# Two heads side by side in the rows of the array: 56-row score products for even and odd heads in place of 72-row products, in an attention and feed-forward kernel on one core

## The reference

```python
x = x + attention(layernorm(x))      # 16 heads of 8 channels, causal,
                                     # T5 relative-position bias (32 buckets, largest distance 128)
x = x + ffn(layernorm(x))            # router fixed to expert 0: relu(t @ w1 + b1) @ w2 + b2,
                                     # residual, layernorm with gamma and beta
# attention: sim = q @ k.T + bias[bucket(i - j)] * scale, -inf above the diagonal; softmax; @ v
```

## Time and profile before

| | us |
|---|---|
| median of 3 runs | 368.16 (365.61 to 368.34) |
| the profiled execution's own time | 367.01 |
| span of its trace | 365.2 |
| PE busy | 326.3 |
| DVE busy | 273.8 |
| ACT busy | 190.4 |
| POOL busy | 65.5 |

### The profile page before, as it was taken

How to read it: one execution, slowest core, us unless ns; L and a number is a source line. 1 busy time by engine, 2 the same in 40 slices (tenths; PEclk the granted TensorE clock), 3 DMA queues, 4 the chain that set the end, 5 groups by cost and what they waited for, 6 DMA issues and landing times.

```text
span 365.2 us, 8215 instructions
## 1 busy us (share of the span) xinstructions
PE 326.3 (89%) x3233; PEld 155.1 (42%) x3235; DVE 273.8 (75%) x952; ACT 190.4 (52%) x262; POOL 65.5 (18%) x79
## 2 busy tenths in 40 slices
PE   8846886699999998998999999899999989999971
PEld 4323442242444354344434434444443443348741
DVE  5565374985777895887799589689969987547895
ACT  1340595134557536655754665574466557763330
POOL 4118999300000000000000000000000001432551
PEclk9985698957999999999999999999999999999997
DMA  7455317200202201020220123032112102000022
GB/s 203 138 176 134 82 46 242 82 4 1 66 2 66 61 9 46 24 66 1 68 63 7 52 48 93 2 90 73 31 55 48 24 3 39 9 2 16 0 57 58
DMA packets 13830, 20.89 MB, mean 57 GB/s; under 512 B 2944, under 2 KB 10240, under 8 KB 13664
## 3 DMA queue, kind: packets, MB, share of 16 engines
q1 hardware_dynamic: 13104, 17.28, 17.4%
q10 hardware_dynamic: 688, 3.09, 3.1%
HBM read 13.90 MB, written 4.23 MB: 50 GB/s over the span
## 4 chain that ended last, share of the span: by engine, by line
PE 58%; DVE 16%; ACT 14%; issue 5%; POOL 3%; DMA 2%; ACTq 1%; DVEq 0%; POOLq 0%
PE ps L1029 15%; PE ps L1072 15%; PE ps L1043 14%; ACT PT L647 10%; PE ps L1060 6%; DVE FM L783 4%; DVE junk L790 3%; PE ps L963 2%; ACT TT L605 2%; POOL XN L495 2%; PE ps L1105 2%; DVE st L858 1%; DVE U L911 1%; DMA qk_scratch<-QS 1%; DMA table_s<-in_table 1%
## 5 line engine op out<-in xcount | busy, mean ns | idle before, releaser
L647 ACT ACTIVATE PT<-ps 128x1024 f32<-128x1024 f32 (+1 forms) x192 | 145.6, 810 | 113.0 <-PE ps L1060 95.0
L783 DVE TENSOR_REDUCE FM<-ps 128x1 f32<-128x512 f32 (+3 forms) x176 | 108.2, 660 | 18.3 <-PE ps L1029 18.2
L790 DVE CUSTOM_DVE_ANT_0 junk<-ps,NBH 128x256 bf16<-128x256 f32 (+1 forms) x256 | 89.5, 403 | 33.9 <-PE ps L1029 33.7
L1029 PE MATMUL ps<-KA,QA 72*128 72x256 bf16 (+3 forms) x544 | 107.2, 291 | 2.2 <-DVE FM L783 1.0
L1043 PE MATMUL ps<-QA,KA 74*128 74x512 bf16 (+3 forms) x384 | 95.7, 334 | 11.1 <-ACT PT L647 9.7
L1072 PE MATMUL ps<-PT,VG 128*16 128x512 f32 (+3 forms) x768 | 86.9, 498 | 0.0
L1029 PEld LDWEIGHTS ps<-KA,QA 72*128 72x128 bf16 x544 | 43.9, 100 | 87.2 <-DVE FM L783 33.1
L541 POOL TENSOR_SCALAR tmp<-mv 128x4 f32<-128x4 f32 x8 | 2.3, 289 | 266.5 <-DVE mv L861 266.5
L1043 PEld LDWEIGHTS ps<-QA,KA 74*128 74x128 bf16 x384 | 31.9, 99 | 36.8 <-ACT PT L647 24.0
L1060 PE MATMUL ps<-TT,flb 128*32 128x176 f16 (+4 forms) x1152 | 38.5, 243 | 0.0
L1060 PEld LDWEIGHTS ps<-TT,flb 128*32 128x32 bf16 x1152 | 21.3, 96 | 17.5 <-issue 16.6
(11 more groups left out here) (93 smaller groups left out, 250.1 us busy)
## 6 DMA issues: line engine op xcount, KB each, us to landing
QA<-qk_scratch SPq DMA_DIRECT2D x48, 96.0 KB
KA<-qk_scratch SPq DMA_DIRECT2D x42, 96.0 KB
qk_scratch<-QS SPq DMA_DIRECT2D x8, 384.0 KB, 4.1
X<-in_x SPq DMA_DIRECT2D x4, 256.0 KB, 5.3
PT<-fr_scratch ACTq DMA_DIRECT2D x1, 1024.0 KB, 4.6
out<-U SPq DMA_DIRECT2D x4, 256.0 KB, 2.3
OT<-f_scratch ACTq DMA_DIRECT2D x2, 480.0 KB, 8.7
xnT<-OT SPq DMA_DIRECT2D x28, 32.0 KB
```

The lines of the kernel that those rows point to most:

```text
L647: nc.scalar.activation(PT[:, s % 3, 2 * q:2 * q + 2, off:off + w], ST[:, q, :, off:off + w], ACT.Exp).then_inc(s_exp, 1)
L783: nc.vector.tensor_reduce(FM[:, ib, heads[0]:heads[-1] + 1, piece], bank[:, 0:w * len(heads)].rearrange("p (h n) -> p h n", n=w), AX.X, AL ...
L790: last = nc.vector.tensor_tensor_reduce(junk[:, k % NSM, i, 0:w], bank[:, i * w:(i + 1) * w], nb[:, h, 256 - w:256], 1.0, NEG, ALU.add, AL ...
L1029: last = nc.tensor.matmul(bank[:, i * w + j - j0:i * w + j - j0 + n], QA[0:KS, p, ib // 4, h, (ib % 4) * 128:(ib % 4 + 1) * 128], KA[0:KS, ...
```

## The change

The rows of the products go from 72 and 74 to 56 and 58: seven of the nine pairs of parts (all three of q with the high and the middle part of k, and the high part of q with the low part of k), and the two maximum rows. Heads 0 and 2 of a group lie in rows 0 to 57, heads 1 and 3 in rows 64 to 121, so each of the two products of a pair uses its own 64-row half of the array. A unit now holds heads of one parity; two units, one of each parity, are one `job`, whose matmuls alternate between the halves and go to two PSUM banks. The job of units k and k+1 waits until unit k - 2 has been read. `NU` becomes 42 (40 units in 20 jobs, and two "m"). The number of DMAs for a half of q or k goes from 3 to 6, and of `move_m` from 1 to 2. `ones` fills all rows of half as many columns.

```diff
-ROWS = NPART * NPART * HD
-KS = ROWS
-MROW = ROWS
+HP = HG // 2
+KS = (NPART * 2 + 1) * HD
+MROW = KS
...
-                nh = min(HG, 512 // pw)
-                for h0 in range(0, HG, nh):
-                    out.append(("far", ib, list(range(h0, h0 + nh)), j0, pw, piece))
-        nh = HG if ib == 0 else 2
-        for h0 in range(0, HG, nh):
-            out.append(("near", ib, list(range(h0, h0 + nh))))
+                nh = min(HP, 512 // pw)
+                for q0 in range(0, HP, nh):
+                    for e in range(2):
+                        out.append(("far", ib, [2 * q + e for q in range(q0, q0 + nh)], j0, pw, piece))
+        for e in range(2):
+            out.append(("near", ib, [2 * q + e for q in range(HP)]))
...
+JOBS = [k for k in range(NU) if UNITS[k][0] == "m" or UNITS[k][2][0] % 2 == 0]
...
-QK_AT = {5: (0, 0), 6: (0, 1), 7: (1, 0), 8: (1, 1)}
+QK_AT = {6: ((0, 0), (0, 1)), 8: ((1, 0), (1, 1))}
...
         def load_q(eng, g, p, c):
-            for u in range(NPART):
-                eng.dma_start(QA[u * NPART * HD:(u + 1) * NPART * HD, p, c, :, :].rearrange("r h n -> r (h n)"),
-                              bass.AP(qk_d, g * GN + 2 * c * NPART * PN, [[HG * IC, HD], [PN, NPART], [1, HG * IC]])
+            at = g * GN + 2 * c * NPART * PN
+            for e in range(2):
+                for u in range(2):
+                    r0 = 64 * e + 24 * u
+                    eng.dma_start(QA[r0:r0 + 24, p, c, :, :].rearrange("r h n -> r (h n)"),
+                                  bass.AP(qk_d, at + e * HP * IC, [[HG * IC, HD], [PN, NPART], [1, HP * IC]])
+                                  ).then_inc(s_ldqk[p][c], 16)
+                eng.dma_start(QA[64 * e + 48:64 * e + KS, p, c, :, :].rearrange("r h n -> r (h n)"),
+                              bass.AP(qk_d, at + e * HP * IC, [[HG * IC, HD], [1, HP * IC]])
                               ).then_inc(s_ldqk[p][c], 16)
...
-                sp.dma_start(QA[MROW:MROW + 2, p, half, :, :], mrow[:, half, :]).then_inc(s_md[half], 16)
+                for e in range(2):
+                    r0 = 64 * e + MROW
+                    sp.dma_start(QA[r0:r0 + 2, p, half, :, :],
+                                 mrow[4 * e:4 * e + 4, half, :]).then_inc(s_md[half], 16)
...
+                pieces = [(i, h // 2, j, n) for i, h in enumerate(u[2]) for j, n in cuts]
+                pe.wait_ge(s_smf, NU * g + k + 2)
+                for m, (i, q, j, n) in enumerate(pieces):
+                    for e in range(2):
+                        last = nc.tensor.matmul(SM[:, (k + e) % NSM, i * w + j - j0:i * w + j - j0 + n],
+                                                QA[64 * e:64 * e + KS, p, ib // 4, q, (ib % 4) * 128:(ib % 4 + 1) * 128],
+                                                KA[64 * e:64 * e + KS, p, j // IC, q, j % IC:j % IC + n],
+                                                start=True, stop=True)
+                        if m == len(pieces) - 1:
+                            last.then_inc(s_smr, 1)
...
-                for h in range(2 * q, 2 * q + 2):
-                    last = nc.tensor.matmul(ST[:, q, h % 2, off:off + w],
-                                            KA[0:KST, p, jb // 4, h, (jb % 4) * 128:(jb % 4 + 1) * 128],
-                                            QA[0:KST, p, ic, h, off:off + w], start=True, stop=not near,
+                for e in range(2):
+                    last = nc.tensor.matmul(ST[:, q, e, off:off + w],
+                                            KA[64 * e:64 * e + KST, p, jb // 4, q, (jb % 4) * 128:(jb % 4 + 1) * 128],
+                                            QA[64 * e:64 * e + KST, p, ic, q, off:off + w], start=True, stop=not near,
```

More of the change, by code:

```diff
@@ L131, in places @@
     costs = [unit_cost(u) for u in UNITS]
-    out, own, done = {}, {}, 0.0
-    for u in range(NU):
-        at = t * (S_START + (S_END - S_START) * done / sum(costs[:-1]))
+    out, own = {}, {}
+    for u in JOBS:
+        at = t * (S_START + (S_END - S_START) * sum(costs[:u]) / sum(costs[:-1]))
         if u == NU - 1:
             at = t * M1_AT
-        done += costs[u]
         s, pos = next((s, pos) for c, s, pos in pts if c > at % t)
@@ L157, in places0 @@
     slots = [(s, pos) for s in range(FIRST_STEP[1] - 1) for pos in range(3)]
-    for u in range(OWN0 + 2, NU - 1):
-        own.setdefault(slots[(u - OWN0 - 2) * len(slots) // (NU - 3 - OWN0)], []).append(u)
+    for u in JOBS:
+        if OWN0 + 4 <= u < NU - 1:
+            own.setdefault(slots[(u - OWN0 - 4) * len(slots) // (NU - 5 - OWN0)], []).append(u)
     own[slots[-1]].append(NU - 1)
-    out[slots[-1]] = list(range(FIRST0))
+    out[slots[-1]] = [u for u in JOBS if u < FIRST0]
     slots = [(s, pos) for s in range(FIRST_STEP[1] - 1, NSTEP) for pos in range(3)]
-    for u in range(FIRST0, NEXT0):
-        out.setdefault(slots[(u - FIRST0) * len(slots) // (NEXT0 - FIRST0)], []).append(u)
+    for u in JOBS:
+        if FIRST0 <= u < NEXT0:
+            out.setdefault(slots[(u - FIRST0) * len(slots) // (NEXT0 - FIRST0)], []).append(u)
     return out, own
@@ L266, in build, with hidden @@
         tT = work[:, 10 * IC:12 * IC].rearrange("p (c n) -> p c n", c=2)
-        hid = [work[:, 0:4 * IC],
-               KA[:, 0:1, :, :, :].rearrange("p o c h n -> p (o c h n)").bitcast(F32)]
+        hid = [work[:, 0:4 * IC]] + [
+            a[:, 0:1, :, :, :].rearrange("p o c h n -> p (o c h n)").bitcast(F32) for a in (QA, KA)]
+        def hidden(c, f):
+            if c % 2 == 0:
+                return hid[0][:, f * IC:(f + 1) * IC]
+            return hid[1 + f // 2][:, (f % 2) * IC:(f % 2 + 1) * IC]
         R = [PT[:, 1, :, :], OT[:, 4:6, :].rearrange("p g (c n) -> p (g c) n", n=IC)]
@@ L798, in unit @@
                     nm = NM[:, half, :]
-                    m0, m1 = (MC[:, half, :, q, :] for q in range(2))
+                    m0, m1 = (MC[:, half, :, :, q, :] for q in range(2))
                     v = 4 * g + 2 * half
@@ L1007, in _, with job @@
                 task_flip(i)
-            def unit(g, p, k):
+            def job(g, p, k):
                 u = UNITS[k]
-                bank = SM[:, k % NSM, :]
-                pe.wait_ge(s_smf, NU * g + k + 1)
                 if u[0] == "m":
-                    half = u[1]
+                    bank, half = SM[:, k % NSM, :], u[1]
+                    pe.wait_ge(s_smf, NU * g + k + 1)
                     pe.wait_ge(s_ms, 2 * g + half + 1)
@@ L1017, in unit @@
                         last = nc.tensor.transpose(bank.bitcast(BF16)[0:8, i * 128:(i + 1) * 128],
[L1018 removed]
+                                                   MC[:, half, i, :, :, :].rearrange("p e q h -> p (e q h)"), idb[:, :])
                     last.then_inc(s_smr, 1)
                     return
[L1021 removed]
+                ib = u[1]
                 if u[0] == "far":
@@ L1127, in s_units_at @@
                     for k in (OWN_UNITS0 if first else OWN_UNITS).get((s, pos), []):
-                        unit(g, p, k)
+                        job(g, p, k)
                     if not last:
@@ L1131, in s_units_at @@
                             if k in HALF_UNITS:
-                                pe.wait_ge(s_ldqk[1 - p][HALF_UNITS[k]], 96 * load)
-                            unit(g + 1, 1 - p, k)
+                                pe.wait_ge(s_ldqk[1 - p][HALF_UNITS[k]], LOADED * load)
+                            job(g + 1, 1 - p, k)
                 for s in range(NSTEP):
@@ L1165, in _ @@
             keep_busy(4, 6)
-            for k in range(OWN0):
+            for k in JOBS[:JOBS.index(OWN0)]:
                 if k in T_AT:
                     task_t(1, T_AT[k])
-                if k in QK_AT:
-                    task_qk(1, *QK_AT[k])
+                for c, qk in QK_AT.get(k, ()):
+                    task_qk(1, c, qk)
                 if k in V_AT:
@@ L1175, in _ @@
                 if k in HALF_UNITS:
-                    pe.wait_ge(s_ldqk[0][HALF_UNITS[k]], 96)
-                unit(0, 0, k)
+                    pe.wait_ge(s_ldqk[0][HALF_UNITS[k]], LOADED)
+                job(0, 0, k)
             pe.wait_ge(s_r, 4)
@@ L1184, in _ @@
                 scores(0, 0, 0, q)
-                unit(0, 0, OWN0 + q)
+                job(0, 0, OWN0 + 2 * q)
             biases(0, 0)
```

43 lines of the change are left out of this document (22 added, 21 removed).

## The result

The changed kernel takes 385.17 us (median of 4 runs, 380.66 to 388.10), the kernel before beside it 367.13. The ratio is 1.045, with a 95% interval of 1.035 to 1.056. The four runs differ in their clock: the mean granted one is 0.929 in the fastest and 0.905 in the slowest. The forecast was 378, with a range of 356 to 391.

What follows compares the result with a forecast made beforehand. PE bounded groups 1 to 5, DVE close. On 367.0 us: start-up +2.0, group 0 -3.0, groups 1 to 5 +3.3, group 6 +2.3, group 7 -2.0, clock +7.2 gave 376.8; 1.2 for the median: 378, range 356 to 391.

Steps and rivals of the forecast that it cites:

- the main case: SP's queue becomes the bound of a group and the clock falls behind it: 372 to 392 us; chance 0.50.
- That the halves don't overlap: Rival: PE's work stays, with the DMA wait on top; 33.5 us a group, 384 us; chance 0.08.
- That SP isn't late: Rival: the twelve DMAs land in time for PE; 30.2 us a group, 356 us (350 to 363); chance 0.18.
- The clock holds: Rival: same DMA wait, but no stretch of low clock; 371 us (365 to 373); chance 0.24.
- the pair's wait: Jobs 12 to 39: each waits until only one unit is unread; DVE starves 0.8 us (bounds 0 and 1.5).
- the walk: Jobs up to T (a group's first exponential), each at the later of PE's turn and its awaited unit; 15.3 us DVE work.
- The stop: PE stands still 2.8 us ahead of job 12 in each group until the twelfth load lands.
- The clock: Granted clock falls behind PE's standstill in each group: 1.2 us a group (ends 0 and 3.5), +7.2 in all.
- Start and group 0: Start-up +2.0 us for three more ACT DMAs; group 0 -3.0 us, its second half freed of PE's bound.
- Group 6: Four reciprocals on DVE, three of them behind the DMA wait: 35.0 us, +2.3, without the clock's 1.2.
- Group 7: No units; its chain runs through scores in 12 steps: -2.0 us (bounds -3 and 0).

Runs made afterwards that it cites:

- the dummies: Ten dummy products of 512 columns on PE ahead of job 12, ahead of the wait for the loads, in the changed kernel: 384.66 us.
- the torn biases: Biases of each pair right behind its scores: 351.23 us on the changed kernel with q loads first, jobs earlier, 7 start dummies; 385.62 us in the kernel before.

## Why the prediction was right, and where its numbers were not

**The mechanism and its place were right.** Twelve issues in 7.7 us behind two for the rows, PE standing still in front of job 12 until a DMA lands, a lower clock behind it, 34.2 us a group where the main case said 33.6 (31.76 + 0.65 + 1.2). The run with the q loads first takes the queue's stop away and gives 12 us back; the run with twice the DMAs puts it into the old kernel and costs 2.1 us in each group with a full clock.

**The rivals.** That the halves don't overlap is out: 0.34 us for two products of 384 columns. That SP isn't late is out as a description of the change; made true, it gives 373 and not the 356 worked out for it. "The clock holds" was true by itself in group 5, which takes 33.4 us where this rival had 32.4; with the dummies it was made true in nearly all groups, at the price of a later job 12, and gives 384.7 and not 371.

**The step that was mis-sized is the one on the pair's wait**, the walk from job 12 to the next T, where "DVE starves 0.1 to 0.3 us at four places, 0.8 in all", and with it the 30.2 us of a group whose loads are in time. That group takes 32.14. The way from job 12 to the next T, 17.1 us in the walk, is 18.3 in group 5 with the clock at 1.00; in group 2 it is 19.4 (159.01 to 178.44), of which the clock is 1.1. That leaves 1.2 us a group that the walk didn't have. Two edits show part of what the walk lacks: VectorE idle in the first steps (0.9 us came back by placing the jobs earlier), and ACT's chain through scores, jobs and biases (2.0 came back by the torn biases). My own reading of the rest, which no run isolates: the walk took each engine's work at its row, and let an engine start as soon as one other was ready; it never let ACT, DVE and PE each be a little late on the same step.

**The stop was over-sized.** The landing was T+14.7, not 15.3, since the issues for 8 rows take 0.46 us and not 0.65; PE came at T+13.3, not 12.5. So the stop is 1.5 us in this group (10.9 us in six), not 2.8. It lengthened a group by about 1.0 us (33.1 against 32.14: a landing at T+14.8 and 18.3 us behind it), where the forecast had 2.2 (32.4 against 30.2). **The clock was right in sum:** 1.1 to 1.2 us in each of groups 1 to 4, nothing in group 5 and 3.1 in group 6, together some 7.6 us where 7.2 were forecast. That it would hold in one group and stay down 10 us in another wasn't foreseen. The walk and the stop err in opposite ways, and it is luck that the sum of a steady group came out near: +2.4 a group measured, +1.85 forecast.

**Start and group 0 went the other way**, +4.8 against -1.0. ACT's three more issues are there (the NBH copy at 26.28 instead of 24.28). But the first exponential is at 62.5 and not 58.2, since the twelve dummies ran at 1.2 GHz for 5.15 us and ended after ACT was ready. From 55 to 60 the granted clock was 0.50. In the run with the q loads first the same program starts at 57.8, so this part isn't the change alone. From the first exponential to its copy group 0 then takes 48.9 us and took 50.4, so it gains 1.5 where 3.0 were forecast. SP's 24 issues did move the stores to 72.6, but not the m1 row: VectorE had `mrow` only at 80.9. **Group 6** cost 5.9 and not 3.5: the clock's 3.1 against 1.2 is most of the difference, and without it the group would be 2.8 longer than before, near the 2.3 forecast. **Group 7** was right (-1.8 against -2.0).

## What to carry to other kernels

When a change takes work from the bound engine, look at what it adds to a queue that is on no chain yet: here six more DMAs on SP let the last load land after PE had come for it (issued at T+12.9, wanted at T+13.3), which cost 2.05 us in a typical group (half of it through the clock), while of PE's 36 us of saved work in the whole kernel next to nothing became time. Free time on the former bound is worth nothing until something spends it; find the edit that was too dear for the full engine (here the torn biases, +2.3 us a group before, -2.0 after) and make it together with the change. When you fill a gap with dummies to price the clock, look when the next real product starts: here the dummies held the clock and hid two thirds of its price by coming too late out of the gap. And a walk along one chain gives a lower end: where three engines work through shared buffers and none of them is full, expect more (here 32.14 us where the walk gave 30.2).

## What the runs showed of the hardware

- A second product in the other 64-row half cost nothing that can be read: 0.34 us for two of 384 columns against 0.33 for one.
- A DMA issue on SP takes 0.65 to 0.67 us for 24 rows (medians), and 0.46 for 8 rows of 2 KB; halving the bytes of the 24 rows changed nothing (0.643 and 0.654 before, 0.652 with twice the DMAs).
- The price of a low clock goes with how long it lasts: 1.1 to 1.2 us for some 3.4 us of it in the changed kernel, 3.1 for some 10 us (group 6), and 4.5 for some 10 us where PE is nearly the bound (the old products with twice the DMAs).
- The length of a stop alone doesn't tell whether the clock falls: in the changed kernel it stayed at 1.00 behind a stop of 1.83 us (group 5) and fell behind one of 1.47 (group 3).
- With 56 instead of 72 rows, products, columns and order unchanged, the clock stayed at 1.2 GHz for some 12 us longer in group 0 of the profiled run (0.50 against 0.97 from 86 to 96, 0.87 against 1.00 from 96 to 106), with PE 10.00 of 10 us busy in the first. One profile shows it, and the four times (374.6 to 379.7 against a median of 367.6) fit it; the cause is open.
